# Counting dense edges in a graph network: one 16-bit table for every four tiles, and work moved to SyncE and GpSimd

## The reference

```python
h = x @ W                                             # first layer
out = segment_sum(h[src] * norm[:, None], dst, N)     # norm from the degrees
x = layernorm(x + out)
# four layers
h = einsum('ni,rio->rno', X, W)
msg = h[etype, src] * inv_deg[:, None]                # 1 / count(dst, etype)
agg = segment_sum(msg, dst, N)
out = elu(layernorm(agg + X @ root + bias) * gamma + beta) + X
# at the end: layernorm(x + out)
```

## Time and profile before

| | us |
|---|---|
| median of 3 runs | 5975.5 |
| lowest and highest | 5961.7 and 5984.08 |
| the profiled execution, its own time | 6039.66 |
| its span, first to last instruction | 6037.9 |
| sort, up to the last sums | 0 to about 818 |
| counting of dense edges | about 837 to 1290 |
| layers | 1290 to 6037.9 |

### The profile page before, as it was taken

The page is one execution under the profiler, slowest core; times in us unless marked ns, Lnnn a source line. Parts: engine busy times, 40 slices in busy tenths (PEclk is TensorE's granted clock), DMA queues, the critical chain, the costliest instruction groups (busy, mean ns, idle before and its releaser), DMA issues.

```text
span 6037.9 us, 75112 instructions
## 1 busy us (share of the span) xinstructions
PE 4706.4 (78%) x19177; PEld 3220.2 (53%) x19177; DVE 3761.0 (62%) x10096; ACT 1426.9 (24%) x3639; POOL 3414.1 (57%) x3405
## 2 busy tenths in 40 slices
PE   5888856778888878888886888887888887777776
PEld 3544422345556546556664656664556564555555
DVE  7988865656666655555564555554555554566665
ACT  1066642125555521111111111111111111100001
POOL 0088840026666656666655666664666664666664
PEclk8999988999999988888988998988988898888888
DMA  1000043124454454444445444445444444444444
GB/s 48 1 1 1 1 140 137 74 63 149 148 161 149 148 169 141 142 142 142 146 134 156 155 145 143 146 145 141 146 146 147 140 155 135 131 132 141 135 132 122
DMA packets 378626, 743.99 MB, mean 123 GB/s; under 512 B 76847, under 2 KB 163457, under 8 KB 378168
## 3 DMA queue, kind: packets, MB, share of 16 engines
q0 software_dynamic: 157920, 405.86, 24.0%
q10 hardware_dynamic: 129600, 235.99, 11.6%
q1 hardware_dynamic: 90776, 98.21, 4.8%
HBM read 636.68 MB, written 102.76 MB: 122 GB/s over the span
## 4 chain that ended last, share of the span: by engine, by line
PE 60%; issue 11%; DVE 11%; another core or an unknown queue 10%; DMA 3%; ACT 3%; DVEq 1%; ACTq 1%; SPq 0%
PE psum L722 21%; PE psum L700 20%; PE psum L757 5%; PE psum L654 4%; DVE arena L1420 3%; PE psum L771 2%; DMA emat<-count_blocks 2%; PE psum L813 2%; DVE arena L1287 1%; PE psum L664 1%; DVE arena L1562 1%; DVE arena L1300 1%; DVE emat L1400 1%; PE psum L667 1%
## 5 line engine op out<-in xcount | busy, mean ns | idle before, releaser
L550 POOL DMA_INDIRECT msg<-h_table,g_rel x1978 | 1892.6, 957 | 1121.3 <-issue 440.9
L1420 DVE TENSOR_TENSOR arena<-arena,psum 128x256 f32 x3090 | 1288.2, 417 | 1563.0 <-PE psum L722 836.4
L722 PE MATMUL psum<-msg,emat 128*128 128x256 f32 x4948 | 1625.0, 421 | 655.7 <-issue 360.6
L722 PEld LDWEIGHTS psum<-msg,emat 128*128 128x128 f32 x4948 | 955.2, 206 | 1154.8 <-issue 923.7
L700 PE MATMUL psum<-arena,emat 128*128 128x256 f32 x3200 | 989.0, 422 | 86.1 <-DMA emat<-count_blocks 72.6
L1400 DVE TENSOR_SCALAR emat<-iota,node,weight 128x128 f32<-128x128 f32 x2472 | 908.2, 368 | 155.9 <-issue 78.8
L550 POOL DMA_INDIRECT msg<-h_table,g_src x496 | 485.8, 979 | 702.2 <-PE psum L722 518.4
L700 PEld LDWEIGHTS psum<-arena,emat 128*128 128x128 f32 x3200 | 667.8, 213 | 251.1 <-issue 148.2
L550 POOL DMA_INDIRECT hout<-h_table,g_rel x494 | 472.7, 957 | 327.5 <-issue 115.4
L532 POOL DMA_INDIRECT placed_rows<-leaving,idx x300 | 439.2, 1464 | 371.3 <-issue 341.7
L722 PE MATMUL psum<-hout,emat 128*128 128x256 f32 x1232 | 410.2, 423 | 161.6 <-issue 72.2
(11 more groups left out here) (249 smaller groups left out, 4746.8 us busy)
## 6 DMA issues: line engine op xcount, KB each, us to landing
emat<-count_blocks ACTq DMA_DIRECT2D x500, 256.0 KB
more_blocks<-count_blocks ACTq DMA_DIRECT2D x250, 256.0 KB
h_table<-hout SPq DMA_DIRECT2D x100, 512.0 KB
count_blocks<-emat ACTq DMA_DIRECT2D x150, 256.0 KB
msg<-h_table,g_rel POOLq DMA_INDIRECT x1978
arena<-h_table SPq DMA_DIRECT2D x24, 512.0 KB
msg<-h_table,g_src POOLq DMA_INDIRECT x496
hout<-h_table,g_rel POOLq DMA_INDIRECT x494
```

The lines of the kernel that those rows point to most:

```text
L550: pool.indirect_dma_start(out=slots[n % RING], out_offset=None, in_=table[:, :], in_offset=bass.IndirectOffsetOnAxis(ap=rows[:, t:t + 1], ...
L722: pe.matmul(agg_ps[n % NPS][:, 0:D], emat[:, n % BODY, :], slots[n % RING], start=True, stop=True).then_inc(s_mm, 1)
L1420: dve.tensor_tensor(a, a, agg_ps[n % NPS][:, 0:D], ALU.add).then_inc(s_acc, 1)
```

## The change

PE's three tables become one, `turns`, of 16-bit values, four for a tile (`after`, the set, the banks to open, the banks to shut); PE loads the sixteen values of four tiles at once, with no bounds check. The offset of a second bank becomes a constant, and the spare banks are two. DVE takes the dense columns apart first, writes the matrices of four tiles, and only then the sparse columns (`sparse_edges`, with a semaphore of its own, `s_sparse`, for the gathers); its wait for `s_inv_b` moves from behind tile 4 to behind tile 3. SP issues the stores of the blocks in place of ACT. GpSimd sets `acc` to zero in place of DVE, ahead of its first gather.

```diff
-        sets_i = hout[0:1, 1, D:D + 2 * DT].bitcast(i32)
-        edges_i = hout[0:1, 3, D:D + 2 * DT].bitcast(i32)
+        turns = hout[0:1, 1, D:D + 2 * DT].bitcast(u16)
...
@@ block.sync
             load_cache(0)
+            for b in range(ND):
+                sp.wait_ge(s_free, b + 3)
+                for k in range(KH):
+                    sp.dma_start(count_dram[b, :, k * R * P:(k + 1) * R * P],
+                                 blocks[b % 2 * KH + k]).then_inc(s_stored[b % 2], 16)
...
@@ block.gpsimd
                 if q == 0:
-                    pool.wait_ge(s_decoded, 1)
+                    pool.wait_ge(s_sparse, 1)
...
+            pool.wait_ge(s_h0, NW)
+            pool.memset(acc, 0.0).then_inc(s_acc, ACC0)
             gather(0, h0_table, g_src)
...
@@ build_counts, on PE
-                        _, after = nc.values_load_multi_w_load_instructions(
-                            after_i[0:1, part], engines=[mybir.EngineType.PE], min_val=1,
-                            max_val=ND)
-                        _, sets = nc.values_load_multi_w_load_instructions(
-                            sets_i[0:1, both], engines=[mybir.EngineType.PE], min_val=0,
...
-                        _, edges = nc.values_load_multi_w_load_instructions(
-                            edges_i[0:1, both], engines=[mybir.EngineType.PE], min_val=0,
+                        few = slice(4 * t, 4 * min(DT, t + FEW))
+                        _, turn = nc.values_load_multi_w_load_instructions(
+                            turns[0:1, few], engines=[mybir.EngineType.PE], min_val=0,
                             max_val=NOWHERE,
...
-                            mm = end_set(bank_at(shut, step, c))
+                            mm = end_set(shut + c * R * P if c else shut)
...
@@ flush_counts, on ACT
                     c.then_inc(s_free, 1)
-                    act.wait_ge(s_free, b + 3)
-                    for k in range(KH):
-                        act.dma_start(count_dram[b, :, k * R * P:(k + 1) * R * P],
-                                      blocks[b % 2 * KH + k]).then_inc(s_stored[b % 2], 16)
...
@@ DVE
             dve.sem_inc(s_decoded, 1)
             dve.wait_ge(s_decoded, 1)
-            dve.wait_ge(s_h0, NW)
-            dve.memset(acc, 0.0).then_inc(s_acc, ACC0)
+
+            def sparse_edges():
+                a_s, b_s, c_s, e_s = (v[:, 0:NT] for v in (a_i, b_i, c_i, e_i))
+                split_values(a_s, b_s, c_s, e_s)
...
-                if t == OH:
+                if t == OH - 1:
+                    sparse_edges()
                     dve.wait_ge(s_inv_b, 16)
```

More of the change, by code:

```diff
@@ L22, in build_program @@
     f32, f16, i32 = mybir.dt.float32, mybir.dt.float16, mybir.dt.int32
+    u16 = mybir.dt.uint16
     ALU = mybir.AluOpType
@@ L59, in build_program @@
     NOWHERE = 2 * AW
+    assert NOWHERE + AW <= 6 * 512
     done_at = [(j + 1) * NT // NW for j in range(NW)]
@@ L222, in build_program @@
         is_new = msg[0:1, 8:12, :].rearrange("p a b -> p (a b)")[:, 0:DT].bitcast(i32)
+        turns_i = msg[0:1, 0:8, :].rearrange("p a b -> p (a b)")[:, 0:4 * DT].bitcast(i32)
+        after_of, set_of, open_of, shut_of = (
+            turns_i.rearrange("p (t v) -> p t v", v=4)[:, :, k] for k in range(4))
         before16 = small(EP, EP // 2 + 1, f16)[:, 0:EP]
@@ L342, in build_program @@
         s_decoded = sem("s_decoded")
+        s_sparse = sem("s_sparse")
         s_oh = sem("s_oh")
@@ L776, in end_set @@
                                  start=False, stop=True)
-            def bank_at(first, step, c):
-                return nc.s_assert_within(first + step * c if c else first, 0, NOWHERE,
-                                          skip_runtime_bounds_check_because="its set or NOWHERE")
             def build_counts():
-                begin_set(NOWHERE)
                 for c in range(KH):
+                    begin_set(NOWHERE + c * R * P)
                     begin_set(c * R * P)
@@ L788, in build_counts @@
                     if k == 0:
[L789 to L799 removed]
+                        few = slice(4 * t, 4 * min(DT, t + FEW))
+                        _, turn = nc.values_load_multi_w_load_instructions(
+                            turns[0:1, few], engines=[mybir.EngineType.PE], min_val=0,
                             max_val=NOWHERE,
[L801 to L803 removed]
+                            skip_runtime_bounds_check_because="a set's number, 0, AW or NOWHERE")
+                    after, at, opened, shut = turn[4 * k:4 * k + 4]
                     if t:
[L805 removed]
+                        pe.wait_ge(s_free, after)
                         for c in range(KH):
[L807 removed]
+                            mm = end_set(shut + c * R * P if c else shut)
                             if c == KH - 1:
                                 mm.then_inc(s_built, 1)
[L810 removed]
+                            begin_set(opened + c * R * P if c else opened)
                     pe.wait_ge(s_oh, t + 1)
@@ L815, in build_counts @@
                                   start=False, stop=False)
-                end_set(NOWHERE)
+                for c in range(KH):
+                    end_set(NOWHERE + c * R * P)
                 for c in range(KH):
```

51 lines of the change are left out of this document (26 added, 25 removed).

## The result

The changed kernel took 6064.57 us (median of 4 runs, 6046.07 to 6077.5), the kernel before, on the same chip, 5979.79 us (4 runs, 5961.7 to 5984.19). The ratio is 1.0142, with a 95% interval from 1.0124 to 1.0159: 1.4% slower, 84.8 us. The forecast was 5875 us, with a range from 5840 to 5915; the time lies 150 us above the end of that range. The profiled execution took 6060.81 us, its span 6058.8.

The account below looks back on a forecast made before the run. PE's queue loading registers was taken as the phase's bound. Savings of 68 us late and 35 early, less 1.5, made 101.5 us, ratio 0.983 to the profiled execution; applied to the median, 5875 us, range 5840 to 5915.

Parts of the forecast that it names:

- The reading of the bound: In the phase of some 450 us, PE's queue loading registers was the bound; 82.2 us of late idle time.
- The piece of the chain: Sign: PE's "issue" ahead of a group's first product, 2.04 us before, should fall below 0.4 us.
- the price of the new load: PE's load of sixteen 16-bit values per four tiles was taken as 0.9 us, the middle of 590 and 1180 ns.
- the upper bound: PE's new load was to cost at most 3.1 us, twice DVE's median of 1538 ns for eight values.
- the load costs by the register, and dearly: Rival: PE's new load takes 3.1 us, the kernel gets slower, near 6010 us, deciding from 2.9 us; chance 0.02.
- The 0.9 us that are hidden: In each group PE's queue starts loading 0.9 us before PE runs dry, so that much of the load is hidden.
- The clock: In the late stretch PE's busy time was taken as 4.4 us a group, at a granted clock of 0.92.
- Dense columns first: At the head of the phase, dense matrices begin some 12 us earlier but gain nothing; the wait moved forward loses 1 us.
- The cover: DVE's wait for `s_inv_b` until 859.06 hides the decoding changes; without it, about 12 us either way.
- GpSimd clears the sums: GpSimd's memset of `acc` ahead of its first gather takes 5.7 us and costs nothing, within DVE's slack.
- Stores on SyncE: Stores moved from ACT to SP gain nothing, one wait replacing another; bounds 16.7 us won or as much lost.
- The layers: Sign: everything behind the phase should last as long as before, 4748 us.

Follow-up runs that it names:

- e7: Kernel before with only the table changed, to 32-bit words, one load of sixteen per four tiles: 5895.59 us against 5977.5, ratio 0.9859.
- e1: Changed kernel with its table in 32-bit words instead of 16-bit values, plus a masking operation per tile: 5215.56 us against 5313.27 for the kernel before, ratio 0.9815.
- e5: Changed kernel with its 16-bit table read as eight 32-bit words and taken apart in registers: 5885.19 us against 5977.5 for the kernel before, ratio 0.9848.
- e8: e1 with VectorE's early windows starting at multiples of four words: 5892.19 us against 5977.5 for the kernel before, ratio 0.9856.
- e3: Kernel before with the 16-bit table alone; stores, clearing and decoding as before: 5401.29 us, ratio 1.0164 to the kernel before.
- e11: e7 with the stores issued by SyncE: 5933.36 us against 6031.66 for the kernel before, ratio 0.984.
- e9: e1 run again as a base on another chip: 5937.91 us against 6031.66 for the kernel before, ratio 0.9845.
- e4: Changed kernel with the three old tables, loads and bounds checks, so everything but the table: 5311.83 us, ratio 0.9996 to the kernel before.

## Why the prediction was wrong, step by step

**The reading of the bound was right.** PE's queue, which loads registers, bounded this phase. With a load of 1.11 us the kernel gains 97.7 us where 101.5 were summed, the phase ends at 1190 where 1188 was said, and the ratio is 0.9815 (0.9845 on another chip) where 0.983 was. A group takes 4.7 us from 1003 on, where 4.6 was said. The piece of the chain fell from 2.04 to 0.6 to 0.9 us; I had said below 0.4. That the sums agree so closely is in part luck: the forecast took all of the gain as idle time of PE from the shorter load, with nothing for the stores. The table of words alone gave 82 us (e7) where 103 were summed for it, and the stores made up for that; and of e1's 100 us in the phase only 69 were idle time, as is said below.

**The step that failed is the price of the new load.** The forecast had "A load of sixteen 16-bit values does not occur", then bounds of 0.334 and 3.1 us, and "The nearest rows are PE's own, so I take the middle of 590 and 1180, 0.9 us". Measured are 4.42 us, above the upper bound. The cost goes neither by bytes (e5: the same 32 bytes in 0.59 us) nor by number alone (e1: sixteen words in 1.11 us). It goes by whether a value is a word and where the load starts: 1.11 / 16 = 0.07 us a value for words from a multiple of 16 bytes, 0.24 to 0.31 for 16-bit values and for words one word off it, by the medians of early and late stretches. The rows of PE from which I took the price had all been aligned words. The row that held the answer was in the document: VectorE's loads of eight words, from 594 to 2516 ns. I used this spread as "eight values cost three engines three different times" and did not ask which of the loads were the long ones. The starts answer it, and e8 confirms it: the long ones started off a multiple of four. The upper bound, too, stood on a number that no load took: 1538 ns is the middle between eleven loads up to 1.24 us and eleven from 1.84 us. Twice the longest one, 2516 ns, would have been 5.0 us, and twice the usual long one, 1.84, would have been 3.7, both beyond the 2.9 us from which the change loses.

**The rival that came true** was "the load costs by the register, and dearly", with a chance of 0.02. Its sign held: it said that 2.9 us decide, and 4.42 is beyond. No run has loads near 2.9 us, so the threshold itself is not shown; nor is the cost one by the register, as e1 shows. Against it I set the 74 ns a register of PE's own eight values, which are words. The Trainium skill (Runtime: NRT & Kernel Launch, Instruction fetch mechanics) gives about 200 ns a register, for loads that this page describes as coming from HBM; the tables here lie in SBUF. The unaligned and 16-bit loads here come near it with 240 to 310, the aligned words do not with 70. By this rival's own working, 4.42 us would have made a gap of 4.42 + 0.1 - 0.9 = 3.6 us in place of 2.04, 100 us on 64 groups, and with its 15 us of waits 6091. The time is 26 us below that. The idle time of PE in the phase grew by 46 us only, and its busy time by 38 at the lower clock. Two things kept the idle time down. The 0.9 us that are hidden were read in one group and taken for all; where the products before ran at 1.2 GHz, 2.2 to 3.7 us of a load were hidden, as shown above. And PE's waits for ScalarE ahead of line 785, 16.7 and 0.7 us before, are 3.9 and 1.8 now; in e3, where ScalarE still issues the stores, they are 20.8 from 860 on. "Issue" ahead of this line grew from 126.1 to 178.2 us, 0.8 us on 64 groups in place of 1.6.

**The clock.** The sum kept PE's 4.4 us of work a group fixed, and a granted clock of 0.92 with it. It moved both ways: PE's busy time in the phase was 338.9 us (clock 0.77 and 0.84), 301.2 (0.84 and 0.92) and 269.9 (0.93 and 1.00) in the changed kernel, the kernel before and e1. So of e1's gain some 31 us are work done faster, and 69 are idle time removed; gaps and clock went the same way each time. e3 against the kernel before shows it with the table alone changed: 336.2 us of busy time at 0.77 and 0.84.

**Dense columns first.** The first set is opened at 832.9 (837.2 before), its first product comes at 838.1 behind a load of 5 us, and VectorE stands still until 859.64, having waited 13.10 us for the inverse counts: 859.06 before, 12.42 us. ScalarE copies its third block at 866.92, after a wait of 21.59 us for a store to land, where it was 862.17 before; yet by 880 both kernels have written 15 tiles. The cover held as said, the gain is nothing, and e11 against e9 shows the same beside a cheap table.

**GpSimd clears the sums.** 5.43 us against the 5.7 predicted. One of VectorE's sparse operations beside it took 5.77 us, where its neighbours of the same width take 0.48, and both began at 837.16, so it looks as if the two engines got into each other's way, inside VectorE's slack. Cost nothing, as forecast.

**Stores on SyncE.** I gave them nothing, between 16.7 us won and as much lost. Beside the old loads that was right (e4: 1.4 us). Beside a cheap load it is 11 to 17 us of phase, up to the upper end of that bound. The mechanism was to be that ScalarE's issues leave the way of its copies; PE's waits for these copies hardly changed, and most of the gain is busy time at a higher clock, so the size agrees and the cause is open. ScalarE's waits for landed stores appeared as well, 23.4 us in the changed kernel in place of 3.9, nearly all of it the one of 21.59 us; they do not eat up the gain.

**The layers.** They were to last 4748 us and lasted 4685. The profiled execution of the kernel before was 1% above its own median, and the medians differ by what the phases do, so the change is not the cause.

The last copy of the phase and the first fetch behind it, the rows that answer to the earlier trace rows, are as far apart as before, 3.7 us:

```profile
1374.49 1.07 ACT L913 COPY emat<-psum 128x512 f32<-128x512 f32 x2 [81.01 <-PE psum L785]
...
1378.22 1.79 ACTq L895 DMA_DIRECT2D emat<-count_blocks  x4
```

## What to carry to other kernels

On TensorE and VectorE a load of registers from a table was cheap only where the values were 32-bit words and the load started at a multiple of 16 bytes; 16-bit values, tried on TensorE, save bytes and took four times as long. If room is short, keep the packed table, load it as words and take them apart in registers (e5). And where the rows nearest to an unknown price have a spread of four times, find out what separates the short from the long ones before taking their middle: the spread was the mechanism.

## What the runs showed of the hardware

- A load of registers (PE's queue), medians: eight aligned words 0.59 us, sixteen 1.11; eight 16-bit values 1.94, sixteen 4.42; sixteen words that start one word off a multiple of 16 bytes 4.42. Before 1000 these were 1.0, 1.7, 2.5, 5.0 and 5.0, and in late groups sixteen 16-bit values took 3.8. On VectorE eight words took 0.59 to 1.24 us from a multiple, 1.84 to 2.52 from one word behind it.
- The same load of 3.78 us left PE idle for 2.95 us where the products before it ran at 2.4 GHz, and for 1.42 where they ran at 1.2.
- A longer gap in TensorE's work cost twice in this phase: the idle time, 46 us more, and 38 us more for the same products at a lower granted clock (0.77 and 0.84, from 0.84 and 0.92). Two products of 512 columns stand 0.85 us apart in the changed kernel's chain, at the level of 1.2 GHz, and 0.43 in that of e1, at 2.4 GHz, where the stretch had a granted clock of 1.00.
- GpSimd's clearing of 6400 columns took 5.43 us, and a VectorE operation on 618 columns that began with it 5.77, where its neighbours took 0.48.
- In e5 PE's busy time was 290 us at the same clocks as e1's 270, with the same products. Busy time with register operations between the products is longer; what part of this is modelled is open.
